# Sixteen-head attention of 16-wide heads in one block, with score rows and keys issued by halves of two heads and outputs packed two units to an array's rows

## What is computed

```
n = layernorm(x)
q, k, v = n @ q_w.T + q_b, n @ k_w.T + k_b, n @ v_w.T + v_b   # 16 heads of 16
q, k = rope(q), rope(k)
probs = softmax(q @ k.T / 4, axis=-1)                          # 512 x 512 per head
x = x + (probs @ v) @ out_w.T + out_b
```

## Time and profile before

| | us |
|---|---|
| median of three runs (2555.74 to 2564.32) | 2562.69 |
| the profiled execution, its own time | 2561.54 |
| its recorded span | 2559.8 |
| TensorE matmul busy (share of span) | 2321.4 (91%) |
| VectorE busy | 1680.6 (66%) |
| ScalarE busy | 1194.9 (47%) |
| GpSimd busy | 1096.8 (43%) |
| layer C, from the barrier ahead of it to the one behind | 1828.3 to 2052.3 |
| of it, main loop from the first shift | 1905.5 to 2036.9 |

### The profile page before, as it was taken

The page is one execution under the profiler, slowest core; times in us unless marked ns, Lnnn a source line. Parts: engine busy times, 40 slices in busy tenths (PEclk is TensorE's granted clock), DMA queues, the critical chain, the costliest instruction groups (busy, mean ns, idle before and its releaser), DMA issues. The chain is left out here.

```text
span 2559.8 us, 49049 instructions
## 1 busy us (share of the span) xinstructions
PE 2321.4 (91%) x18400; PEld 1610.1 (63%) x18400; DVE 1680.6 (66%) x3286; ACT 1194.9 (47%) x2936; POOL 1096.8 (43%) x1267
## 2 busy tenths in 40 slices
PE   7888898888988889888769999999899989999999
PEld 4577655776557865677646666676443456666685
DVE  7677686776867768678647777732367567777613
ACT  5644465554655546554434555422125445555411
POOL 0477534774347743477525544420130035444300
PEclk9999999999999999999989999998899999999999
DMA  2100001000010000000031000000100040000000
GB/s 64 37 2 3 2 17 38 2 2 2 18 38 2 2 2 17 17 2 2 2 96 34 19 20 19 1 1 1 51 1 1 1 123 19 15 18 13 1 1 17
DMA packets 57640, 46.29 MB, mean 18 GB/s; under 512 B 11576, under 2 KB 50880, under 8 KB 57024
## 3 DMA queue, kind: packets, MB, share of 16 engines
q1 hardware_dynamic: 57408, 43.16, 5.8%
HBM read 42.10 MB, written 1.05 MB: 17 GB/s over the span
## 5 line engine op out<-in xcount | busy, mean ns | idle before, releaser
L1265 DVE SCALAR_TENSOR_TENSOR work<-four,taps,work 128x511 f32<-128x511 f32 (+2 forms) x384 | 284.1, 747 | 78.7 <-ACT work L912 69.5
L1883 POOL TENSOR_TENSOR rot<-q_plain,ropes 128x512 f32<-128x512 f32 x64 | 81.0, 1265 | 534.6 <-ACT q_plain L1914 534.6
L624 PE MATMUL four<-xT,wring 128*128 128x512 f32 x512 | 254.5, 625 | 0.2 <-DVE work L1265 0.2
L979 ACT ACTIVATE work<-four 128x512 f32<-128x512 f32 x216 | 129.0, 597 | 267.5 <-PE four L734 241.1
L785 PE MATMUL four<-work 128*128 128x128 f32 x1536 | 215.6, 284 | 0.0
L1927 ACT ACTIVATE pr<-four,nmaxf 128x512 f32<-128x512 f32 (+3 forms) x256 | 134.0, 525 | 170.8 <-DVE nmaxf L1769 170.8
L1769 DVE TENSOR_REDUCE nmaxf<-four 128x1 f32<-128x512 f32 (+3 forms) x256 | 125.8, 491 | 125.7 <-PE four L1612 121.7
L785 PEld LDWEIGHTS four<-work 128*128 128x128 f32 x1536 | 191.9, 195 | 3.9
L1610 PE MATMUL four<-rot,rot 128*128 128x512 f32 (+3 forms) x512 | 178.7, 445 | 5.1 <-DVE rot L1761 3.5
L1190 POOL TENSOR_TENSOR work<-work 128x256 f32<-128x256 f32 x184 | 139.9, 761 | 100.0 <-PE bank L819 90.3
L1183 POOL TENSOR_TENSOR work<-work 128x256 f32<-128x256 f32 x184 | 146.0, 793 | 78.7 <-DVE work L1341 55.8
(11 more groups left out here) (283 smaller groups left out, 5417.4 us busy)
## 6 DMA issues: line engine op xcount, KB each, us to landing
wqkv<-in_f_wq_dram SPq DMA_DIRECT2D x32, 128.0 KB, 2.2
wqkv<-in_f_wk_dram SPq DMA_DIRECT2D x32, 128.0 KB, 2.4
wqkv<-in_f_wv_dram SPq DMA_DIRECT2D x32, 128.0 KB, 2.3
wo<-in_f_wo_dram SPq DMA_DIRECT2D x2, 2048.0 KB, 11.8
we<-in_f_we_dram SPq DMA_DIRECT2D x4, 1024.0 KB
wring<-in_Wk_dram SPq DMA_DIRECT2D x4, 512.0 KB, 3.8
wring<-in_Ww_dram SPq DMA_DIRECT2D x4, 512.0 KB, 5.6
wring<-in_Wv_dram SPq DMA_DIRECT2D x4, 512.0 KB, 3.7
```

The lines of the kernel that those rows point to most:

```text
L624: last = nc.tensor.matmul(unit_bank(i)[:], wring[n % 2][:, c, h * P:(h + 1) * P], k.xT[:, c, b * T:(b + 1) * T], start=(c == 0), stop=(c = ...
L1265: ins = nc.vector.scalar_tensor_tensor(out=cbuf[i % 4][:, n:], in0=unit_bank(i)[:, 0:T - n], scalar=taps[:, {"q": 0, "k": 1}.get(kind, 2), ...
```

## The change

- Layer C's weights (`FullWeights`) are loaded at the end of SyncE's list of layer B; only the rope tables (two loads of 512 KB) and two biases are still loaded in layer C.
- The separate normalisation block is gone; its steps stand at the head of the main block. The second half of the tokens is transposed after the first two projections. `c_o_even` and its clearing are gone.
- `fetch_root_table` takes a square root of one column at the end of ScalarE's list of layer B and of layer C.
- Score rows are issued and their maxima taken for two heads at a time; keys go in the order 2, 3, 0, 1, so that rows of heads 0, 1 stand beside keys of heads 2, 3 and the other way round; `weigh` is split into two halves of 256 columns.
- Two units' outputs are packed into one 128-row group, so `c_oT` and `c_wout` are half as large, every second unit has no second transposition, and the output projection adds up 2 matmuls per tile rather than 4.

```diff
+def fetch_root_table(k, warm):
+    k.nc.scalar.activation(warm[:], k.eye[:, 0:1], ACT.Sqrt)
...
 def expert_block(k, rep, rows=None, stored=None, ahead=None):
...
                     load(head)
+                if ahead is not None:
+                    ahead.load(sp)
...
                     hidden(n)
+                if ahead is not None:
+                    fetch_root_table(k, ahead.warm)
...
+PAIRS_C = ((0, 1), (2, 3))
+KEY_HEADS = (2, 3, 0, 1)
...
-            RING += [("keys", _n - 1, _r, _h) for _h in range(4)]
+            RING += [("keys", _n - 1, _r, _h) for _h in KEY_HEADS]
...
+    def load(self, sp):
+        d, landed = self.d, self.landed
+        for dst, src in ((self.qk[0], "b_q_w"), (self.qk[1], "b_k_w"), (self.v, "b_v_w"), (self.out, "b_out_w")):
+            sp.dma_start(dst[:], d[src].rearrange("(c p) n -> p c n", p=P)).then_inc(landed, 16)
...
+                turn_norm(0)
+                pe.wait_ge(c_in, 112)
                 project(0)
                 for i in range(NPART):
                     if i + 1 < NPART:
                         project(i + 1)
+                    if i == 0:
+                        turn_norm(1)
...
-                def score_rows(n, r):
+                def score_rows(n, r, pair):
                     b, j = UNITS_C[n]
-                    pe.wait_ge(maxed, n * CH + r)
-                    for h in range(4):
+                    if n * CH + r:
+                        pe.wait_ge(maxed, 2 * (n * CH + r - 1) + pair + 1)
+                    for h in PAIRS_C[pair]:
...
-                def weigh(n, r):
+                def weigh(n, r, side):
...
+                    columns = slice(side * T // 2, (side + 1) * T // 2)
                     for h in range(4):
...
                 for n in range(NC_UNITS + 1):
                     for r in range(CH):
-                        if 0 < n < NC_UNITS:
-                            score_rows(n, r)
+                        more = 0 < n < NC_UNITS
+                        if more:
+                            score_rows(n, r, 0)
+                            if r == 0:
+                                score_rows(n, r, 1)
                         if n:
-                            score_keys(n - 1, r, range(RING_BANKS))
+                            score_keys(n - 1, r, KEY_HEADS[:2])
                             if r:
-                                weigh(n - 1, r - 1)
+                                weigh(n - 1, r - 1, 0)
                             elif n >= 2:
-                                weigh(n - 2, CH - 1)
-                            score_keys(n - 1, r, range(RING_BANKS, 4))
+                                weigh(n - 2, CH - 1, 0)
+                        if more and r:
+                            score_rows(n, r, 1)
+                        if n:
+                            score_keys(n - 1, r, KEY_HEADS[2:])
+                            if r:
+                                weigh(n - 1, r - 1, 1)
+                            elif n >= 2:
+                                weigh(n - 2, CH - 1, 1)
...
-                    for j in range(BT):
-                        last = nc.tensor.matmul(k.bank[t % 4][:, 0:D], oT[:, j, t * P:(t + 1) * P], wout[:, j, :], start=(j == 0), stop=(j == BT - 1))
+                    for j in range(BT // 2):
+                        last = nc.tensor.matmul(k.bank[t % 4][:, 0:D], oT[:, j, t * P:(t + 1) * P], wout[:, j, :], start=(j == 0), stop=(j == BT // 2 - 1))
...
                 def maximum(n, r):
-                    dve.wait_ge(rows_made, n * CH + r + 1)
+                    for pair, heads in enumerate((slice(0, 2), slice(2, 4))):
+                        dve.wait_ge(rows_made, 2 * (n * CH + r) + pair + 1)
...
+                        nc.vector.tensor_reduce(out, four[:, heads], AX.X, ALU.max, negate=True).then_inc(maxed, 1)
...
-                    nc.vector.transpose(oT[:, j, b * T:(b + 1) * T], o_even[:]).then_inc(o_kept, 1)
+                    if side:
+                        dve.wait_ge(o_scaled, n + 1)
+                        nc.vector.transpose(oT[:, j // 2, b * T:(b + 1) * T], o_pair[:]).then_inc(o_kept, 1)
```

More of the change, by code:

```diff
@@ L1467, in hidden_done, with expert_block @@
     return max(n for n, unit in enumerate(HIDDEN) if unit[0] == e) + 1
-def expert_block(k, rep, rows=None, stored=None):
+def expert_block(k, rep, rows=None, stored=None, ahead=None):
     nc, d = k.nc, k.d
@@ L2077, in full_attention, with _, turn_norm @@
         with nc.Block() as block:
+            @block.sync
+            def _(sp):
+                for m in range(2):
+                    sp.dma_start(brope[:, 2 * m:2 * m + 2], d["c_brope"][:, 2 * m:2 * m + 2]).then_inc(rope_in[m], 16)
+                for dst, name in ((bv, "b_v_b"), (bout, "b_out_b")):
+                    sp.dma_start(dst[:], d[name].rearrange("(a n) -> a n", a=1).broadcast_to([P, D])).then_inc(bias_in, 16)
             @block.tensor
             def _(pe):
-                pe.wait_ge(c_in, 160)
+                def turn_norm(half):
+                    pe.wait_ge(n_tile, 4 * half + 4)
+                    for c in range(DC):
+                        for t in range(4):
+                            last = nc.tensor.transpose(k.bank[DC * half + c][:, t * P:(t + 1) * P],
+                                                       nrm[:, 4 * half + t, c * P:(c + 1) * P], k.eye[:])
+                        last.then_inc(n_turned, 1)
                 def project(i):
                     j, m, b = parts[i]
+                    pe.wait_ge(n_kept, DC * b + DC)
                     if i >= 2:
@@ L2111, in _ @@
                         pe.wait_ge(c_roped, 2)
-                        score_rows(0, FIRST_ROWS[i])
+                        for pair in range(2):
+                            score_rows(0, FIRST_ROWS[i], pair)
                 for t in range(NT):
@@ L2145, in score_keys @@
                                          shifted[n % 2][rows, :], start=True, stop=True).then_inc(keys_made, 1)
-                def weigh(n, r):
+                def weigh(n, r, side):
                     b, j = UNITS_C[n]
-                    if r == 0:
-                        pe.wait_ge(o_turned, n)
-                    pe.wait_ge(exped, n * KEY_UNITS + 4 * r + 4)
+                    if side == 0:
+                        if r == 0:
+                            pe.wait_ge(o_turned, n)
+                        pe.wait_ge(exped, n * KEY_UNITS + 4 * r + 4)
+                    columns = slice(side * T // 2, (side + 1) * T // 2)
                     for h in range(4):
                         rows = slice(HEAD_ROWS * h, HEAD_ROWS * (h + 1))
-                        last = nc.tensor.matmul(k.bank[7][rows, :], v[:, b * CH + r, 4 * j + h, :], pT[(4 * r + h) % PT_RING][:],
-                                                start=(r == 0), stop=(r == CH - 1))
-                    last.then_inc(weighed, 1)
+                        last = nc.tensor.matmul(k.bank[7][rows, columns], v[:, b * CH + r, 4 * j + h, :], pT[(4 * r + h) % PT_RING][:, columns],
+                                                start=(r == 0 and side == 0), stop=(r == CH - 1 and side == 1))
+                    if side:
+                        last.then_inc(weighed, 1)
                 def shift(n):
@@ L2193, in _, with keep_norm @@
             def _(act):
-                act.wait_ge(c_in, 160)
+                def keep_norm(half):
+                    for c in range(DC):
+                        act.wait_ge(n_turned, DC * half + c + 1)
+                        nc.scalar.activation(k.xT[:, c, half * 512:half * 512 + 512], k.bank[DC * half + c][:], ACT.Copy).then_inc(n_kept, 1)
+                act.wait_ge(n_var, 1)
+                nc.scalar.activation(k.rstd[:], k.rstd[:], ACT.Sqrt).then_inc(n_root, 1)
+                keep_norm(0)
+                act.wait_ge(c_in, 112)
                 for n in range(NPART):
+                    if n == 2:
+                        keep_norm(1)
                     j, m, b = parts[n]
@@ L2311, in build @@
             k.free_sems(kept)
+        weights = FullWeights(k)
         if "B" in layers:
-            expert_block(k, 0)
+            expert_block(k, 0, ahead=weights)
         if "C" in layers:
-            full_attention(k)
+            full_attention(k, weights)
         if "D" in layers:
```

167 lines of the change are left out of this document (58 added, 109 removed).

## The result

The changed kernel takes 2543.82 us (median of 6 runs, 2529.49 to 2546.95), the kernel before, beside it on the same chip, 2561.48 (6 runs, 2553.43 to 2564.32). The ratio is 0.9933 [0.9917, 0.9948]: 17.2 us less, between 13 and 21. A second measurement on another chip gave 2540.86 against 2555.40, ratio 0.9942 [0.9922, 0.9963]. The profiled execution is the quickest of the six: 2529.49, span 2527.7. A barrier's time is the start of SyncE's first load behind it.

A forecast was written before the change was run, and what follows sets the result against it. Layers run serially; layer C was held by late loads, loop waits on maxima and exponentials, and TensorE in the output projection. −8.3 − 4.1 − 4.4 − 1.0 = −17.8 from 2561.5 gives 2543.7; with the median 1.15 higher, 2545 (range 2535 to 2557).

The forecast's parts named there:

- Start of C: Layer C's start: first projection at 1833.2, not 1842.38 (−9.2 us); −8.3 with later transpositions and clock, bounds −5 and −10.
- the table fetch: Start of C: table load moved behind layer B's last GELU, so the square root starts about 1.0 us earlier.
- Projections: First projection to first shift: eight transpositions now in TensorE's path +1.0 us, lower-clock stretch −0.1.
- more is won at the clock: Rival, chance 0.13: value-phase matmuls keep full clock, up to 3 us, and another 3 at the start; then 2539.
- Main loop: Layer C's loop with halved rows, maxima and weigh: unit 16.26 to 15.9 us, −4.1 in all.
- the ring: Main loop: with three key banks, a pair's second key waits for the previous pair's first exponential, 1.81 us after that key.
- the maximum at its end: Main loop: each shift waits for the last two rows' maximum, 0.7 us later than TensorE would be free.
- the pair: Main loop: two heads' phase and half weigh take 1.72 us on the mean, a step 3.44.
- The slower rival: Main loop, chance 0.05: keys start only after two heads' rows stream out, 0.85 us more per pair; +31, so 2576.
- The rival of a dearer half weigh: Main loop, chance 0.13: half weigh with drain costs 0.77, not 0.57, pair 1.82; +9 us, so 2554.
- Output projection: Layer C's end: TensorE needs half per tile, VectorE becomes the bound; seven intervals from 1.69 to 1.06 us, −4.4.
- Start of D: Layer D's start: table load hidden behind the last exponentials, −1.0 us.

The follow-up runs named there:

- Experiment 1: Changed kernel with GpSimd's clearing in layer C held until VectorE has normalised all eight tiles: first projection 4.92 us behind the barrier, C 205.65, run 2540.89 us.
- experiment 7: Changed kernel with layer C's weights loaded in layer C again, ahead of the rope tables: first projection 8.37 us behind the barrier, C 209.24, run 2539.36 us.
- Experiment 8: Changed kernel without the two early square roots that fetch the table: C 209.22 us, first projection of D 6.21 behind its barrier, run 2529.79 us.
- experiment 12: Changed kernel with the late clearing and the weights loaded in layer C again, ahead of the rope tables: first projection 8.12, C 209.09, run 2543.55 us.
- experiment 10: Changed kernel with the late clearing and the first unit's score rows one part earlier: C 205.08 us, median 2541.79, ratio to the kernel before 0.9946.
- experiment 11: As experiment 10, with the normalised input also transposed tile by tile: first projection 3.91, loop 135.62, C 212.26, total 2540.63 us, ratio 0.9942.
- experiment 5: Changed kernel with main-loop exponentials over only 256 of each 512 columns (work left out): pair 1.64 us, loop 122.58, C 204.72, run 2530.84.
- experiment 6: Changed kernel with maxima over only 256 of each head's 512 score columns (work left out): unit 15.49 us, loop 123.37, C 202.38, run 2532.90.
- experiment 3: Changed kernel with keys in order 0, 1, 2, 3, on the same array rows as the score rows ahead of them: unit 19.81, loop 152.85, run 2569.11 us.

## Why the prediction was right, and where it was not

The total (2545 forecast, 2543.8 measured) and the sign are right, and the loop, the output projection and the table load gained by the mechanisms given. That the total came so close is in good part luck. The start of C missed its forecast by 3.5 us, the loop by 0.9 and the start of D by 0.4; the projections made good 1.8 of it, the output projection 0.6 and the rest of D 1.65, for which nothing was forecast.

**Start of C, the failed step.** The prediction moved GpSimd's clearing from 1836.15 to 1828.4, wrote that it "is done by 1833", and costed it at nothing because nobody needs the cleared tile. It looked only for who waits for the clearing, not for what runs beside it. Experiment 1 shows what stood in its place: 3.45 us of VectorE's path. Without that the start is worth 14.02 − 4.92 = 9.1, and the forecast was 9.2; the square root, transpositions and copies then stand as worked out. By the Trainium skill (SBUF — State Buffer, Who interferes with whom) VectorE and GpSimd share one pair of ports; a tensor_scalar can run in a mode that takes it, and whichever instruction starts first holds it to its end. The trace agrees: the clearing starts 0.04 ahead and the addition ends 0.03 behind it.

**The terms of the start were not additive.** The prediction gave the table fetch about 1.0 and the loads the rest. Experiments 7, 8 and 12: in the changed kernel, each of the two taken back alone costs 0 (8.37 and 8.37 against 8.37), because the hold on VectorE covers both. What C's start gained, 5.65, needs only that the path be free of loads before 8.3 and of the table before 3.5. The prediction also did not part two things in the loads. Before, the projection waited for all ten: turn_m was the last, issued at 1834.09 (5.73 behind the barrier) behind the rope table of 1024 KB, and it landed 8.2 later. In experiment 12 all the loads are in C again, but the rope tables and two biases stand behind turn_m and are not waited for (and `c_wout` is half as large), and the projection, again held by turn_m, comes at 8.12. So of the 9.1 us of a start without the hold, 14.02 − 8.12 = 5.9 come, by this comparison, from what is waited for and in which order, and 3.2 from loading ahead of the barrier.

**Projections, +0.9 forecast, −0.9 measured.** Two stretches at the restart of TensorE, and at the value phase, of the changed kernel:

```profile
1821.70:1831.70 10.00, 10.00 (x25) 4.93 (x26) 1.39 (x2) 3.04 (x5) 2.65 (x3) 0.80 0.00 0
...
1875.50:1883.87 8.37, 7.14 (x25) 5.61 (x25) 3.43 (x17) 0.00 (x0) 2.26 (x3) 0.80 0.01 2
```

and of the kernel before:

```profile
1842.40:1852.40 10.00, 10.00 (x17) 4.31 (x18) 1.77 (x3) 2.06 (x3) 2.81 (x3) 0.73 0.00 0
...
1892.40:1905.48 13.08, 9.32 (x30) 7.05 (x29) 7.02 (x20) 0.00 (x0) 5.89 (x8) 0.74 0.01 1
```

From the first projection to the start of the value phase it is 49.23 before (1891.61 − 1842.38) and 49.38 after (1871.08 − 1821.70): +0.15. The eight transpositions are in it, at 0.87 (1827.18 to 1828.05, full clock), and the first 10 us ran at 0.80 instead of 0.73, which gives back 0.7: TensorE now restarts with the first transpositions at 1818.95, so 2.75 us of the stretch at the lower level lie ahead of the first projection. The value phase, with the same 3.24 us wait ahead of its larger part, took 12.79 instead of 13.87. So a third of the rival "more is won at the clock" came true, 1.1 of its 3 in the value phase. It is not tied to the length of the wait alone: the 24 matmuls took 8.22 before and 7.13 after, each behind 3.24, and 7.13 or 5.45 behind 2.57 in experiments 10 and 11. What decides between them stays open.

**Main loop, −4.1 forecast, −3.2 measured.** The mechanism stands with its parts: half weigh 0.57, phase 1.07 where nothing is waited for, half maximum 1.23 (1.22), last unit −1.26 (−1.2), first −0.55 (−0.7). Experiments 5 and 6 show the two limits where they were put: the ring within a unit, the maximum at its end. What was mis-sized is the pair, 1.74 and not 1.72 (the ring's round takes 1.85 and not 1.81, the pair without a wait 1.64 and not 1.62), and so the unit, 16.03 and not 15.9; six units give −1.35, not −2.2. The slower rival (rows and keys do not overlap) needed 31 us; experiment 3, which makes it happen, cost 26. Its place and nearly its price were right, and it is not what this kernel does. The rival of a dearer half weigh falls with the measured 0.57.

**Output projection, −4.4 forecast, −5.0 measured.** VectorE is the bound as said; its pace was mis-sized by taking 1.06 from a place with one operand more. Here it is 0.98.

**Start of D, −1.0 forecast, −0.64 measured.** Experiment 8 shows the fetch worth 0.97, as forecast. The 0.33 that is missing is the clock of the first transpositions. In the kernel before, and in the changed one (stretches from the first transposition to the first copy of the input):

```profile
2055.59:2056.47 0.88, 0.88 (x6) 0.88 (x7) 0.88 (x4) 0.00 (x0) 0.00 (x0) 0.73 1.00 186
```

```profile
2024.86:2026.07 1.21, 1.21 (x6) 1.21 (x7) 1.21 (x5) 0.00 (x0) 0.00 (x0) 0.50 0.75 207
```

Before, TensorE had idled 4.69 us and began at 0.73; now it has idled 5.62, at 0.50. It is through with the output projection sooner than VectorE, and so it stands longer before D. Without the fetch (6.59 idle) it is 0.50 and 1.21 as well, and 6.21 against 5.88 is again 0.33. The prediction costed the faster output projection without what its longer idle time costs behind the barrier.

**The rest of D, 0 forecast, −1.65 measured.** Its code is the same in both. The two profiles differ in one stretch, 16.6 and 16.0 us behind the barrier of D, before and after:

```profile
2068.87:2074.07 5.20, 5.20 (x11) 2.32 (x11) 2.39 (x6) 1.45 (x4) 0.00 (x0) 0.67 1.10 336
```

```profile
2038.53:2042.05 3.52, 3.52 (x10) 1.64 (x11) 1.93 (x5) 1.88 (x5) 0.00 (x0) 1.00 1.10 377
```

That is 1.68 at the lower clock, and behind it 485.68 and 485.65 remain. All of D took 507.44 before, in the one profile that there is, and 505.00 to 506.80 in the thirteen of the changed kernel and its variants, so part of the 1.65 may be scatter.

**The median.** Stage by stage the changes sum to −14.73 − 0.64 − 1.65 = −17.0. The ratios say −17.2 [−13, −21] and, on the second chip, −14.8 [−9, −20]: the stages are inside both.

**A better version.** Moving the clearing (experiment 1) takes 3.57 us from layer C, the first rows one step earlier another 0.6. By the profile, that beats both kernels; in the totals, 2540.89 and 2541.79 beside 2540.86 for the changed kernel, they cannot be told from it.

## What to carry to other kernels

When work moves earlier on an engine whose result nobody is waiting for, ask what runs beside it on other engines, above all a GpSimd clearing next to a VectorE tensor_scalar on SBUF: the page shows the held instruction as busy, so a duration far over that of its twin elsewhere (3.50 against 0.17) is the sign. Two covers over the same wait must be taken away together to see what either is worth; one at a time both read as nothing. And when totals scatter by more than the term in question, compare stages from barrier to barrier, which repeated here to 0.03 us for layer C.

## What the runs showed of the hardware

1. **A GpSimd clearing holds a VectorE tensor_scalar on SBUF to its own end.** 128x4096 f32 cleared in 3.51 us; VectorE's addition over 128x8, begun 0.04 later, took 3.50 and ended with it, in nine profiles of this study 3.49 or 3.50. With the clearing moved (experiments 1, 10, 11, 12): 0.17. It does not hold every operation: the reciprocal at 1817.14 ran beside the next clearing (1816.78 to 1817.33) and took 0.20, as in the kernel before, where GpSimd was idle.
2. **Switching between tiles of 32 array rows and tiles of 32 columns costs some 0.14 us one way and 0.22 us the other.** The weigh of 256 columns takes 0.57 from its load to the next rows, that of 512 columns 1.00: the difference is two passes of 256 columns, so 0.43, and 0.57 − 0.43 = 0.14 remains. Keys or rows with 0.85 us of columns take 1.07 up to the weigh: 0.22.
3. **The clock can fall while TensorE is shown busy.** In experiment 11 the granted clock fell between 2003 and 2004 (0.77 in that microsecond) with PE busy 1.00 of 1.00 there and in the microsecond before; it had been busy 0.37, 0.35 and 0.86 in the three from 1999 to 2002, around the last shift. It stayed at 0.50 between 2010 and 2020 with PE busy 10.00 of 10.00, doing key matmuls and weighs of 32 rows or 32 columns alone. The last unit of the changed kernel has the same wait at its shift, was granted 1.00 (1996 to 2012) and took 15.61; it took 15.62 in every other run with that last unit. What sets this off was not found.
4. **Time at the lower clock outside the edited layer makes the totals scatter.** Up to layer C TensorE has the same work in all these programs, yet its barrier lay anywhere from 1812.57 to 1831.85 us. The two profiled executions of the changed kernel differ by 17.3 us in total, 17.2 of it ahead of C's barrier (1813.33 and 1830.57), with 15128 matmuls in each up to there and a mean granted clock of 0.98 and 0.97: by the traces' clock records 78.5 and 119.5 us at the lower level. Over all fourteen profiles that time and the barrier's place go together, from 75.1 us at 1812.57 on, though not strictly one to one (116.0 at 1831.85).
